# Guest matmuls cut in halves, batch loops written out, and VectorE's guests moved between scans in a fused Mamba and attention kernel

## The chip, the cores and the metric

The kernel runs on 1 core of a Trainium2 chip. The metric is the device time of one execution in microseconds (us). The kernel before takes 3528.84 us, the median of three runs (3526.27 to 3528.93).

## What is computed

For each of B = 4 batches of a sequence x[512, 256], all in fp32:

```
h, gate = adaLN(x, c)                                  # layer norm, scale, shift
for each direction (forward, backward):
    xs, z = split(h @ in_w);  xs = silu(xs)            # 512 channels
    dt, B, C = split(xs @ xproj_w); dt = softplus(dt + dt_bias)
    hst[t] = hst[t-1] * exp(dt[t] * A) + dt[t] * xs[t] * B[t]   # 512 channels x 64 states
    y[t]   = sum over states of hst[t] * C[t];  y = (y + xs * D) * silu(z)
x = x + gate * (y_fwd @ out_w + y_bwd @ out_w)
x = x + gate * (silu(h @ w1) * (h @ w2)) @ w3           # h = adaLN(x, c)
x = x + gamma1 * attention(adaLN(x)) @ proj             # 16 heads, l2-normed q and k
x = x + gamma2 * gelu(adaLN(x) @ fc1) @ fc2
```

## The kernel before

The five engines each run one instruction list, and semaphores set the order between them; every order below is written out by hand. Each of the five runs `batch(b, False)` in a hardware loop `Fori(0, B - 1)` (three turns) and then `batch(B - 1, True)` once, written out. Inside the loop a wait compares with a register value; in the written-out batch it compares with a constant. `wait_over` is a semaphore that only gets incremented behind some waits.

**A batch.** It begins with the scan stage: 128 rows, 64 states forward (d = 0) and 64 backward (d = 1). A row is one state of all 512 channels, as four tiles k = 0..3 of 128 channels by 512 time steps. Per row:
- ScalarE (`feed_scan`, L637 to L643) makes three 128x512 pieces of the inflow and one small diagonal, then four decay tiles exp(dt * A).
- TensorE (`turn_inflow`, L851, L852) turns the inflow of tile k into a PSUM bank (two banks, so it waits until scan k - 2 is over), then `sum_up` (L860) adds the weighed states of the tile six places back into the output banks.
- VectorE (`scan_row`, L1226) runs the scan of each tile, four per row.
- GpSimd (`weigh`, L531) multiplies two scanned tiles at a time by the row of C, twice per row. C's rows come by DMA from SyncE's queue, two states at a time.

States and decays have two slots of a row each, so VectorE can be at most about two pairs of tiles ahead of GpSimd.

**Guests.** While the scan of one direction runs, the next direction's inputs are prepared in its rows. The tuples at the top say in which row s (0 to 63) of a direction each step stands: TensorE's guest matmuls of 512 columns in rows IN_AT (16 rows), C_AT (4 rows, 64 channels wide) and DT_AT (16 rows), one in each row; the B projection in rows 48 to 51, the turns of dtx in rows 52, 55, 56, 58. TensorE does its guest behind tile k == 1 of the row. VectorE's guests stand in 17 rows (L1175 in TANH_AT, L1178 in row 26, L1182 in DT_CAP_AT, L1187 in DT_READY_AT), behind all four scans of their row. GpSimd has four guests per direction (L514, DTX_AT). The last direction of the last batch prepares nothing.

**Look-ahead.** In the forward rows of the three looped batches the next batch's first layer norm is done as well (`look_ahead`): statistics in rows 8 to 11, x_norm in rows 16 to 19 (L1209, a tensor_scalar from SBUF to SBUF), a shift in row 25.

**After the scan** come the Mamba output, MLP, attention and a second MLP, with no scan beside them; a batch ends with an add on VectorE (L1139) and SyncE's store of `out` (L484). SyncE then issues the next batch's first rows of C (L415).

The functions that the diff touches, and their callers:

Of the kernel before, what the change touches and what calls it, by code (L numbers as in the profile page):

```python
# [11 lines left out]
P = 128  # L12
# [100 lines left out]
def build(nc, inp, out):  # L113
    ctx = ExitStack()
    with ctx:
# [122 lines left out]
        wait_over = sem("wait_over")  # L238

# [147 lines left out]
        def _(sp):  # L387
# [18 lines left out]
            def spill(n):  # L406

                sp.wait_ge(c_t_ready, n + 1)
                sp.dma_start(c_spill[bass.ds(n, 1)].rearrange("a m h (j l) -> (a m h j) l", l=L), c_t[:]).then_inc(c_spilled, 16)

            def spread_rows(b, r):
# [4 lines left out]
                             c_spill[bass.ds(n, 1), m, half, :].partition_broadcast(P)).then_inc(c_loaded[half], 16)  # L416
# [21 lines left out]
            def batch(b, last):  # L438

                for r in range(0, BATCH_ROWS, HALF):  # L440
                    d, at = r // NS, r % NS
                    if at == 0:
                        sp.wait_ge(c_spilled, (b * 2 + d + 1) * 16)
                        sp.sem_inc(wait_over, 1)
# [5 lines left out]
                    if d == 0 and at == 6:  # L450
                        sp.dma_start(gate[:].rearrange("p g d -> p (g d)"),
                                     gate_spill[bass.ds(b, 1), :].rearrange("b d -> (b d)").partition_broadcast(P)).then_inc(gate_loaded, 16)
                    if at == 30 and (d == 0 or not last):
                        spill(b * 2 + d + 1)
                    if at == 24 and (d == 0 or not last):
                        sp.wait_ge(in_mm, (b * 2 + d + 2) * 2 * KI)
                        sp.sem_inc(wait_over, 1)
# [5 lines left out]
                    if at == 54 and (d == 0 or not last):  # L463
                        sp.wait_ge(b_tok_mm, b * 2 + d + 2)
                        sp.sem_inc(wait_over, 1)
# [7 lines left out]
                if not last:  # L473

                    sp.wait_ge(lanes_turned, (b + 1) * NG)
                    sp.sem_inc(wait_over, 1)
# [9 lines left out]
            with sp.Fori(0, B - 1) as b:  # L486
                batch(b, False)
            batch(B - 1, True)
# [4 lines left out]
        def _(pool):  # L493
# [44 lines left out]
            def batch(b, last):  # L538
# [9 lines left out]
                pool.sem_inc(wait_over, 1)  # L548
                pool.memset(qk_pad[:], 0.0).then_inc(pads_zero, 1)
                pool.wait_ge(pads_zero, b + 1)  # L550
                pool.sem_inc(wait_over, 1)
# [8 lines left out]
            with pool.Fori(0, B - 1) as b:  # L560
                batch(b, False)
            batch(B - 1, True)


        @block.scalar
        def _(act):
# [7 lines left out]
            def ln(b, i):  # L574
# [4 lines left out]
                act.activation(h_t[:, 1, :], banks[1], ACT.Identity, bias=mod[:, i, SHIFT, 1, bass.ds(b, 1)],  # L579
                               scale=mod[:, i, SCALE, 1, bass.ds(b, 1)]).then_inc(ln_ready, 1)  # L580
# [37 lines left out]
            def look_ahead(b, s):  # L618

                if s == AHEAD_SHIFT_AT[1]:  # L620
                    act.wait_ge(ahead_turned, (b + 1) * KD)
                    act.activation(h_ssm[:, 1, :], guest[0], ACT.Identity, bias=mod[:, 0, SHIFT, 1, bass.ds(b, 1)],
                                   scale=mod[:, 0, SCALE, 1, bass.ds(b, 1)]).then_inc(h_high_ready, 1)
# [81 lines left out]
            with act.Fori(0, B - 1) as b:  # L705
                batch(b, False)
            batch(B - 1, True)
# [3 lines left out]
        def _(pe):  # L711
# [41 lines left out]
            def prepare(n, d, s, ahead=None, first=False):  # L753

                if s in IN_AT:
                    at = IN_AT.index(s)
                    m, kc = at // KD, at % KD
                    if at == 0:
                        pe.wait_ge(in_loaded, 16 * KD * (n + 1))
                    if kc == 0 and m < 2:  # L760
# [13 lines left out]
                    last = pe.matmul(guest[m % 2], lhs, rhs, start=(kc == 0), stop=(kc == KD - 1))  # L774
                    if kc == KD - 1:
                        last.then_inc(in_mm, 1)
                if s in C_AT:
                    kc = C_AT.index(s)
                    if kc == 0:
                        pe.wait_ge(xproj_loaded, 16 * KI * (n + 1))  # L780
                        pe.wait_ge(in_ready, n * 2 * KI + 2 * KI - 1)
                    last = pe.matmul(guest[0][0:NS, :], xproj_w[:, kc, DI + NS:DI + 2 * NS], xs[:, kc, :],
                                     start=(kc == 0), stop=(kc == KI - 1))
                    if kc == KI - 1:
                        last.then_inc(c_mm, 1)
                for m in range(KI):
                    if s in DT_AT[m]:
                        kc = DT_AT[m].index(s)
                        if kc == 0:
# [8 lines left out]
                            else:  # L798
                                pe.wait_ge(dt_ready, n * KI + m - 1)
                        last = pe.matmul(guest[(m + 1) % 2], xproj_w[:, kc, m * P:(m + 1) * P], xs[:, kc, :],  # L800
                                         start=(kc == 0), stop=(kc == KI - 1))
                        if kc == KI - 1:
                            last.then_inc(dt_mm, 1)
                if s in B_TOK_AT:
# [605 lines left out]
```

## Time and profile before

| | us |
|---|---|
| median of three runs | 3528.84 |
| the profiled execution | 3529.55 |
| its span, first to last instruction | 3527.8 |
| PE, DVE, ACT, POOL busy | 3275.1, 2823.1, 2734.3, 2487.5 |

PE is TensorE's matmul, PEld its weight load, DVE VectorE, ACT ScalarE, POOL GpSimd, SP SyncE. In a row of a timeline the second number is the length of the group from its first start to its last end, and the bracket tells how long the engine sat idle before it and what it waited for. Neighbouring instructions overlap slightly in the records, so rates are taken from start to start. The scan stages run from about 99 to 749, 966 to 1616, 1833 to 2484 and 2692 to 3317 us of the span. The mean granted TensorE clock is 0.963.

### The profile page before, as it was taken

The page shows a single profiled execution, that of the slowest core. Times are in us where ns is not written, and L with a number is a line of the kernel's source. Part 1 is how long each engine was busy: PE and PEld are TensorE (multiplying, and loading weights), DVE is VectorE, ACT ScalarE, POOL GpSimd, SP SyncE. Part 2 cuts the span into 40 slices and gives each one's busy share as a digit, 9 for nine tenths or more (in the row PEclk, how much of TensorE's full clock was granted, in tenths as well). Part 3 has the DMA queues.
Part 4 walks back from the last instruction along what each step waited for, and adds up shares of the span by engine and source line. Part 5 has one row for each costly group of instructions (what it writes and reads, how often), then busy time and mean ns, then how long its engine had stood idle before and what let it go on. Part 6 is the DMA issues. An engine that isn't in the chain of part 4 may idle for free.

```text
span 3527.8 us, 68244 instructions
## 1 busy us (share of the span) xinstructions
PE 3275.1 (93%) x22944; PEld 2605.5 (74%) x22944; DVE 2823.1 (80%) x3001; ACT 2734.3 (78%) x4713; POOL 2487.5 (71%) x1103
## 2 busy tenths in 40 slices
PE   7999999988799999998979999999798999999888
PEld 4778888864488888886458788888546888888744
DVE  2899999956299999995639999999455999999653
ACT  1989999952498999993349999999146999999523
POOL 1789999950098999993019999999203999999600
PEclk9999999997999999999889999999989999999989
DMA  3221212100111121110011211212002211111000
GB/s 127 82 68 49 70 55 68 60 26 13 48 65 62 55 70 54 63 67 25 1 59 60 68 53 66 67 57 67 13 1 75 66 56 61 60 55 57 29 13 7
DMA packets 56732, 186.83 MB, mean 53 GB/s; under 512 B 6577, under 2 KB 12721, under 8 KB 55473
## 3 DMA queue, kind: packets, MB, share of 16 engines
q1 hardware_dynamic: 56370, 182.26, 15.3%
q8 instruction: 195, 3.19, 0.4%
q14 instruction: 167, 1.37, 0.1%
HBM read 179.08 MB, written 3.16 MB: 52 GB/s over the span
## 4 chain that ended last, share of the span: by engine, by line
POOL 47%; issue 25%; PE 24%; DVE 3%; DMA 1%; POOLq 0%; ACT 0%; SPq 0%; DVEq 0%; ACTq 0%
POOL states L531 45%; PE bank L993 3%; PE bank L860 3%; PE bank L851 3%; PE bank L900 2%; PE bank L1012 2%; PE bank L1074 2%; PE bank L1024 2%; PE bank L852 1%; PE bank L774 1%; PE bank L800 1%; POOL part L514 1%; PE bank L963 1%; PE bank L736 0%; PE bank L944 0%
## 5 line engine op out<-in xcount | busy, mean ns | idle before, releaser
L531 POOL TENSOR_TENSOR states<-states,c_rows 128x1024 f32<-128x1024 f32 x1024 | 2401.5, 2380 | 566.3 <-DMA c_rows<-c_spill 293.0
L1226 DVE TENSOR_TENSOR_SCAN states<-decay,bank 128x512 f32<-128x512 f32 x2048 | 2336.4, 1201 | 152.8 <-PE bank L852 106.1
L643 ACT ACTIVATE decay<-dt,a_log 128x512 f32<-128x512 f32 x2048 | 1305.5, 710 | 0.0
L860 PE MATMUL bank<-ident,states 128*128 128x128 f32 x8192 | 1240.5, 275 | 34.6 <-POOL states L531 11.9
L851 PE MATMUL bank<-ident,inflow_tok 128*128 128x128 f32 x6144 | 1070.3, 283 | 63.1 <-DVE states L1226 54.3
L637 ACT ACTIVATE inflow_tok<-dtx_tok,b_tok 128x512 f32<-128x512 f32 x1536 | 995.3, 712 | 134.7 <-PE bank L852 134.2
L860 PEld LDWEIGHTS bank<-ident,states 128*128 128x128 f32 x8192 | 952.5, 142 | 76.7 <-POOL states L531 73.4
L851 PEld LDWEIGHTS bank<-ident,inflow_tok 128*128 128x128 f32 x6144 | 686.7, 141 | 361.6 <-issue 127.1
L852 PE MATMUL bank<-b_diag,dtx_tok 128*128 128x128 f32 x4096 | 794.5, 276 | 0.0
L852 PEld LDWEIGHTS bank<-b_diag,dtx_tok 128*128 128x128 f32 x4096 | 621.3, 192 | 0.0
L638 ACT ACTIVATE b_diag<-ident,b_tok 128x128 f32<-128x128 f32 x512 | 199.3, 389 | 0.0
L1313 DVE TENSOR_REDUCE decay<-bank 128x1 f32<-128x512 f32 x256 | 159.0, 684 | 46.2 <-PE bank L993 45.7
L558 POOL TENSOR_TENSOR states<-inflow_tok 128x512 f32<-128x512 f32 x16 | 16.7, 1041 | 240.3 <-DVE inflow_tok L1280 240.3
L993 PE MATMUL bank<-dtx_tok,dt 32*128 32x512 f32 x512 | 169.4, 808 | 6.8 <-DVE decay L1313 3.7
L693 ACT ACTIVATE y_gated<-bank 128x512 f32<-128x512 f32 x176 | 91.7, 601 | 63.5 <-PE bank L1012 63.5
L1012 PE MATMUL bank<-dt,dtx_tok 32*128 32x512 f32 x512 | 130.6, 673 | 0.0
L800 PE MATMUL bank<-xs,xproj_w 128*128 128x512 f32 x256 | 128.7, 594 | 0.0
L993 PEld LDWEIGHTS bank<-dtx_tok,dt 32*128 32x128 f32 x512 | 72.6, 230 | 67.0 <-DVE decay L1313 42.8
L1161 DVE TENSOR_TENSOR dt<-bank,row_b 128x512 f32<-128x512 f32 x16 | 11.0, 687 | 126.0 <-PE bank L900 126.0
L577 ACT ACTIVATE std<-var_eps 128x4 f32<-128x4 f32 x12 | 2.5, 205 | 141.0 <-DVE var_eps L1125 141.0
L749 PE MATMUL bank<-ident,x_norm 128*128 128x128 f32 x96 | 23.0, 413 | 60.0 <-DVE x_norm L1130 60.0
L1012 PEld LDWEIGHTS bank<-dt,dtx_tok 32*128 32x128 f32 x512 | 53.6, 199 | 26.0 <-issue 10.8
(143 smaller groups left out, 1968.6 us busy)
## 6 DMA issues: line engine op xcount, KB each, us to landing
c_rows<-c_spill SPq DMA_DIRECT2D x256, 512.0 KB, 3.7
xproj_w<-in_xproj_w SPq DMA_DIRECT2D x32, 320.0 KB, 4.3
in_w<-in_in_w SPq DMA_DIRECT2D x16, 512.0 KB, 4.8
in_w<-in_fc_w SPq DMA_DIRECT2D x8, 512.0 KB, 5.3
xproj_w<-in_w SPq DMA_DIRECT2D x8, 512.0 KB, 5.0
xproj_w<-in_fc_w SPq DMA_DIRECT2D x4, 1024.0 KB, 4.8
y_gated<-in_mod_w SPq DMA_DIRECT2D x1, 2048.0 KB, 7.6
x_ahead<-in_x SPq DMA_DIRECT2D x4, 512.0 KB, 5.1
```

The lines of the kernel that those rows point to most:

```text
L531: pool.tensor_tensor(pair, pair, c_row, ALU.mult).then_inc(weighed, 1)
L637: act.activation(inflow_tok[:, r % SLOTS, t, :], dtx_tok[:, d, t, :], ACT.Copy, scale=b_tok[:, d, t, s:s + 1])
L638: act.activation(b_diag[:, r % SLOTS, :], ident[:], ACT.Copy, scale=b_tok[:, d, TT - 1, s:s + 1]).then_inc(inflow_tok_ready, 1)
L643: act.activation(decay[:, r % SLOTS * KI + k, :], dt[:, d, k, :], ACT.Exp, scale=a_neg[:, d, k, s:s + 1]).then_inc(decay_ready, 1)
L800: last = pe.matmul(guest[(m + 1) % 2], xproj_w[:, kc, m * P:(m + 1) * P], xs[:, kc, :], start=(kc == 0), stop=(kc == KI - 1))
L851: pe.transpose(to[:, t * P:(t + 1) * P], inflow_tok[:, r % SLOTS, t, k * P:(k + 1) * P], ident[:])
L852: pe.matmul(to[:, (TT - 1) * P:TT * P], dtx_tok[:, d, TT - 1, k * P:(k + 1) * P], b_diag[:, r % SLOTS, :], start=True, stop=True).then_inc ...
L860: last = pe.matmul(banks[KI + t][:, k * P:(k + 1) * P], states[:, r % SLOTS * KI + k, t * P:(t + 1) * P], ident[:], is_transpose=True, sta ...
L993: pe.matmul(score_bank(u), q_t[a, g, t * P:(t + 1) * P], k_t[a, g, :], start=True, stop=True).then_inc(scores_mm, 1)
L1012: pe.matmul(banks[S_BANKS + v % T_BANKS], k_t[a, g, kt * P:(kt + 1) * P], q_t[a, g, :], start=True, stop=True).then_inc(scores_t_mm, 1)
L1226: dve.tensor_tensor_scan(states[:, slot, time], decay[:, slot, time], banks[k % INFLOW_BANKS][:, time], 0.0, ALU.mult, ALU.add).then_inc(s ...
L1313: dve.tensor_reduce(qk_pad[:, t, g, lane:lane + 1], score_bank(u), AX.X, ALU.min).then_inc(neg_ready, 1)
```

## The change

Four edits:
- TensorE's guest matmuls of 512 columns become two of 256. The first half is issued behind tile k == 1 and the second behind k == 3 of the same row; waits stay with the first half, the semaphore with the second. The B projection, the turns of dtx and of x_norm stay whole, behind k == 1.
- VectorE's scan guests and look-ahead stand between scan 1 and scan 2 of their row, no longer behind scan 3. The y gating of direction 0 stays behind all four scans.
- The look-ahead's x_norm is a scalar_tensor_tensor, with rstd as a broadcast SBUF tensor.
- All batches are written out on all engines; `wait_over` is gone.

```diff
-                with pe.Fori(0, B - 1) as b:          # and the same on SP, POOL, ACT, DVE
-                    batch(b, False)
-                batch(B - 1, True)
+                for b in range(B):
+                    batch(b, b == B - 1)
...
+            def halves(to, lhs, rhs, h, start, stop):
+
+                out = None
+                for half in h:
+                    c = slice(half * L // 2, (half + 1) * L // 2)
+                    out = pe.matmul(to[:, c], lhs, rhs[:, c], start=start and half == 0, stop=stop, skip_group_check=True)
+                return out
...
-                    last = pe.matmul(guest[m % 2], lhs, rhs, start=(kc == 0), stop=(kc == KD - 1))
-                    if kc == KD - 1:
+                    last = halves(guest[m % 2], lhs, rhs, h, kc == 0, kc == KD - 1)
+                    if kc == KD - 1 and 1 in h:
                         last.then_inc(in_mm, 1)
...
+                    if k % 2 and (d == 0 or not last):
+                        prepare(b * 2 + d + 1, 1 - d, s, (k // 2,), b + 2 if d == 0 and not last else None)
                     if k == 1:
-                        if d == 0 or not last:
-                            prepare(b * 2 + d + 1, 1 - d, s, b + 2 if d == 0 and not last else None)
                         if d == 0 and not last:
                             look_ahead(b + 1, s, b * 2 + 1)
...
-                    dve.tensor_scalar(x_norm[:, t, :], x_ahead[:, t, :], mean_var[:, t, 0:1], rstd[:, t:t + 1],
-                                      ALU.subtract, ALU.mult).then_inc(ahead_norm, 1)
+                    dve.scalar_tensor_tensor(x_norm[:, t, :], x_ahead[:, t, :], mean_var[:, t, 0:1],
+                                             rstd[:, t:t + 1].to_broadcast([P, D]), ALU.subtract,
+                                             ALU.mult).then_inc(ahead_norm, 1)
...
-                    scan_row(b, r)
-                    if d == 1 and s == 0:
-                        gate_rows(b, 0)
+                    scan_row(b, r, range(0, PAIR))
                     if d == 0 or not last:
...
                         prepare(b * 2 + d + 1, 1 - d, s)
                     if d == 0 and not last:
                         look_ahead(b + 1, s)
+                    scan_row(b, r, range(PAIR, KI))
+                    if d == 1 and s == 0:
+                        gate_rows(b, 0)
```

## Rows read from the trace of the kernel before

**Rows 1.** The page, costliest group: count | busy, mean ns | idle before.

```profile
L531 POOL TENSOR_TENSOR states<-states,c_rows 128x1024 f32<-128x1024 f32 x1024 | 2401.5, 2380 | 566.3 <-DMA c_rows<-c_spill 293.0
```

**Rows 2.** Windows: stretch, its length; PE, PEld, DVE, ACT, POOL busy (x); clock, DMA.

```profile
3020.00:3310.00 290.00, 276.18 (x2254) 249.03 (x2254) 287.04 (x250) 284.33 (x491) 287.45 (x124) 1.00 0.16 56
1305.00:1612.00 307.00, 301.70 (x2356) 259.29 (x2355) 290.81 (x266) 294.37 (x510) 294.12 (x128) 1.00 0.18 60
```

**Rows 3.** Windows of line 1226 alone: each from scan 0 of row 3 to row 52.

```profile
983.22:1236.29 253.07, 223.29 (x197) 0.99 0.17 60
1311.19:1556.33 245.14, 222.35 (x198) 1.00 0.17 58
2708.88:2956.05 247.17, 222.80 (x197) 1.00 0.18 61
```

**Rows 4.** Timeline of DVE, looped batches: start us, us, instructions [idle <-releaser].

```profile
215.47 4.55 DVE L1226 TENSOR_TENSOR_SCAN states<-decay,bank 128x512 f32<-128x512 f32 x4 [0.78 <-PE bank L852]
...
1341.43 6.77 DVE L1226 TENSOR_TENSOR_SCAN states<-decay,bank 128x512 f32<-128x512 f32 x6
...
1443.88 4.55 DVE L1226 TENSOR_TENSOR_SCAN states<-decay,bank 128x512 f32<-128x512 f32 x4 [0.49 <-PE bank L852]
...
1455.61 0.72 DVE L1182 TENSOR_SCALAR part<-bank,dt_b 128x512 f32<-128x512 f32 x1
1456.26 11.21 DVE L1226 TENSOR_TENSOR_SCAN states<-decay,bank 128x512 f32<-128x512 f32 x10
```

**Rows 5.** Timeline of DVE, the written-out last batch.

```profile
2837.57 4.55 DVE L1226 TENSOR_TENSOR_SCAN states<-decay,bank 128x512 f32<-128x512 f32 x4 [0.55 <-ACT decay L643]
```

**Rows 6.** Timeline of PE around one guest matmul, last batch.

```profile
2744.93 0.30 PEld L774 LDWEIGHTS bank<-in_w,h_ssm 128*128 128x128 f32 x2
...
2745.90 0.49 PE L851 MATMUL bank<-ident,inflow_tok 128*128 128x128 f32 x3
...
2746.89 0.49 PE L851 MATMUL bank<-ident,inflow_tok 128*128 128x128 f32 x3
```

**Rows 7.** Lines by form: GpSimd's guest, and the look-ahead's x_norm.

```profile
L514 POOL TENSOR_TENSOR part<-dt,xs 128x512 f32<-128x512 f32 x32 | 41.2, 1288 | 38.2 <-DVE dt L1187 38.2
...
L1209 DVE TENSOR_SCALAR x_norm<-x_ahead,mean_var,rstd 128x256 f32<-128x256 f32 x16 | 17.4, 1102 | 1.2 <-POOL rstd L520 1.2
```

**Rows 8.** Timeline of DVE and POOL at the look-ahead's x_norm, first batch.

```profile
205.78 2.22 DVE L1209 TENSOR_SCALAR x_norm<-x_ahead,mean_var,rstd 128x256 f32<-128x256 f32 x1
...
193.34 14.52 POOL L531 TENSOR_TENSOR states<-states,c_rows 128x1024 f32<-128x1024 f32 x6 [2.47 <-DVE states L1226]
```

**Rows 9.** Timeline of DVE and SP where batch 1 and batch 3 begin.

```profile
957.04 0.69 DVE L1139 TENSOR_TENSOR part<-part,x_norm 128x512 f32<-128x512 f32 x1
965.52 2.33 DVE L1226 TENSOR_TENSOR_SCAN states<-decay,bank 128x512 f32<-128x512 f32 x2 [7.79 <-issue]
...
958.24 0.42 SPq L484 DMA_DIRECT2D out<-part  x1
965.23 0.99 SPq L415 DMA_DIRECT2D c_rows<-c_spill  x2
...
2691.02 0.69 DVE L1139 TENSOR_TENSOR part<-part,x_norm 128x512 f32<-128x512 f32 x1
2691.63 5.66 DVE L1226 TENSOR_TENSOR_SCAN states<-decay,bank 128x512 f32<-128x512 f32 x5
```

**Rows 10.** Timeline of DVE: the last scans of batches 0 and 3, and the last add.

```profile
740.12 4.75 DVE L1226 TENSOR_TENSOR_SCAN states<-decay,bank 128x512 f32<-128x512 f32 x4
...
3307.37 5.67 DVE L1226 TENSOR_TENSOR_SCAN states<-decay,bank 128x512 f32<-128x512 f32 x5 [0.36 <-ACT decay L643]
...
3523.68 0.69 DVE L1139 TENSOR_TENSOR part<-part,x_norm 128x512 f32<-128x512 f32 x1
```

**Rows 11.** Timeline of ACT and DVE: one tanh and the instruction that reads it.

```profile
1349.23 0.58 ACT L597 ACTIVATE part<-bank 128x512 f32<-128x512 f32 x1
...
1355.38 0.66 DVE L1175 SCALAR_TENSOR_TENSOR xs<-part,bank 128x512 f32<-128x512 f32 x1
```

More of the change, by code:

```diff
@@ L558, in batch @@
                     pool.tensor_tensor(qk_sq[:, t, :], qk[:, t, :], qk[:, t, :], ALU.mult).then_inc(sq_ready, 1)
-            with pool.Fori(0, B - 1) as b:
-                batch(b, False)
-            batch(B - 1, True)
+            for b in range(B):
+                batch(b, b == B - 1)
         @block.scalar
@@ L703, in batch @@
                     act.activation(gelu_h[:, m, :], banks[m], ACT.Gelu, bias=fc1_b[:, m:m + 1]).then_inc(fc1_ready, 1)
-            with act.Fori(0, B - 1) as b:
-                batch(b, False)
-            batch(B - 1, True)
+            for b in range(B):
+                batch(b, b == B - 1)
         @block.tensor
@@ L751, in ln, with prepare @@
                 pe.wait_ge(ln_ready, (n + 1) * KD)
-            def prepare(n, d, s, ahead=None, first=False):
+            def halves(to, lhs, rhs, h, start, stop):
[4 more added lines that the diff above has]
+                return out
+            def prepare(n, d, s, h=(0, 1), ahead=None, first=False):
                 if s in IN_AT:
@@ L778, in prepare @@
                     kc = C_AT.index(s)
-                    if kc == 0:
+                    if kc == 0 and 0 in h:
                         pe.wait_ge(xproj_loaded, 16 * KI * (n + 1))
                         pe.wait_ge(in_ready, n * 2 * KI + 2 * KI - 1)
-                    last = pe.matmul(guest[0][0:NS, :], xproj_w[:, kc, DI + NS:DI + 2 * NS], xs[:, kc, :],
-                                     start=(kc == 0), stop=(kc == KI - 1))
-                    if kc == KI - 1:
+                    last = halves(guest[0][0:NS, :], xproj_w[:, kc, DI + NS:DI + 2 * NS], xs[:, kc, :], h, kc == 0, kc == KI - 1)
+                    if kc == KI - 1 and 1 in h:
                         last.then_inc(c_mm, 1)
@@ L799, in prepare @@
                                 pe.wait_ge(dt_ready, n * KI + m - 1)
-                        last = pe.matmul(guest[(m + 1) % 2], xproj_w[:, kc, m * P:(m + 1) * P], xs[:, kc, :],
-                                         start=(kc == 0), stop=(kc == KI - 1))
-                        if kc == KI - 1:
+                        last = halves(guest[(m + 1) % 2], xproj_w[:, kc, m * P:(m + 1) * P], xs[:, kc, :], h, kc == 0,
+                                      kc == KI - 1)
+                        if kc == KI - 1 and 1 in h:
                             last.then_inc(dt_mm, 1)
+                if 0 not in h:
+                    return
                 if s in B_TOK_AT:
@@ L1079, in batch @@
                 residual_rows(lambda c, t: gelu_h[:, c, t * P:(t + 1) * P], lambda c: fc2_w[:, c, :], KF)
-            with pe.Fori(0, B - 1) as b:
-                batch(b, False)
-            batch(B - 1, True)
+            for b in range(B):
+                batch(b, b == B - 1)
         @block.vector
@@ L1342, in batch @@
                 residual(b, 3, GAMMA2, FC2_B)
-            with dve.Fori(0, B - 1) as b:
-                batch(b, False)
-            batch(B - 1, True)
+            for b in range(B):
+                batch(b, b == B - 1)
 def kernel(**inputs):
```

42 lines of the change are left out of this document (17 added, 25 removed).

## The prediction, made blind

> **What bounds the kernel now.** I read the page first. GpSimd's weighing, 1024 times 2.38 us, is 2401.5 of 3527.8 us [rows 1], and the chain of waits names it for most of the scan. The windows show where it really is the bound. In the last direction, which has no guests, POOL is busy for 287.45 of 290 us with 124 weighings: 290/124 = 2.34 us each, 4.67 us a row [rows 2]. That is the floor of a row, and GpSimd's four guests of 1.29 us add about 5 us to each of the seven directions that prepare the next one [rows 7]. In such a direction POOL is busy only 294 of 307 us [rows 2].
>
> To see who holds it there I cut windows on VectorE's scans, 49 rows (3 to 51): 253.07 us forward with look-ahead, 245.14 backward, both in looped batches, and 247.17 in the written-out batch [rows 3]. The floor would be 49 x 4.67 + 5 = 234. VectorE's timeline explains the rest. Ten scans with nothing between take 11.21 us, 1.11 from start to start (a record overlaps the next by 0.08), so an empty row is 4.45 [rows 4], below the floor. To that come:
> - its own guest, 0.58 (0.66 less the overlap) [rows 11] or 0.65 for dt [rows 4];
> - a wait where TensorE's guest matmul was ahead of scan 2: 0.49 idle in the loop, hence a row of 4.55 + 0.49 = 5.04; 0.78 where the matmul is 64 channels wide, 5.33 [rows 4]; 0.55 in the written-out batch, 5.10 [rows 5].
>
> With both, a row is 5.6 to 5.7. But the six scans from 1341.43 go through without an idle time [rows 4], though the first four are row 9, which has a guest matmul: VectorE's guest at the end of row 8 gave TensorE 0.58 us to run ahead. So today a VectorE guest covers the TensorE guest of the next row, in nine rows of a direction (4, 9, 12, 17, 20, 27, 35, 42, 44), and by the same the B projection in 48 and 51.
>
> **Halves.** A half costs half. In the written-out batch the guest's weights load at 2744.93 and the next tile's matmuls start at 2745.90, 0.97 later, while two weight loads take 0.30 and the following tile comes 0.99 after [rows 6]. A tile costs TensorE 0.99 at full speed, and I put the guest at 0.86 and a half at 0.43. The whole guest of 0.86 delays the scan by 0.55 + 0.08 = 0.63, so 0.23 is slack and a half should delay it by 0.20. Two halves by VectorE: 4.45 + 0.40 = 4.85. By TensorE: 4 x 0.99 + 0.86 = 4.82. I take 4.82. Bounds: 4.67, the floor, if the slack takes them whole, and 5.10 if the second costs as much as the first saves.
> The 64-channel matmul delays by 0.78 + 0.08, 0.29 more than the 0.57 of the others in the loop. I take this as fixed for each insertion, so that two halves give a TensorE row of 4 x 0.99 + 0.86 + 0.58 = 5.40, nothing won.
>
> **VectorE's guests between scans 1 and 2.** They now stand where the first half's delay falls, and leave TensorE time for the second. A row with both guests becomes 4.45 + 0.58 = 5.03 (dt: 5.10). The price is the cover of the next row: those nine rows go from about 4.46 to 4.82, and 48 and 51 to 5.1.
> GpSimd gets its second pair later by the guest. That costs nothing where VectorE is the slower one, and its lead of up to two pairs covers it elsewhere. What the guests read is there: a tanh of ScalarE ends at 1349.81 and is read at 1355.38 [rows 11], and reading two scans (2.2 us) sooner, with the matmul's last half about 2.2 later, leaves over 1 us. ScalarE is busy 294 of 307 us already [rows 2], so it would be late next.
>
> The ledger of 49 rows, without look-ahead: 8 rows with a guest of 0.58 (TensorE's hidden) 40.2; 8 with one of 0.65, 40.8; row 22 (both, 64 channels) 5.3; 20 with halves only 96.4; 3 with 64-channel halves only 16.2; 3 with the B projection only, uncut, 15.3; 6 empty 26.8. Sum 241.0, above the floor of 234.
> - Three looped backward directions (I take the measured one for all): 245.14 - 241.0 = 4.14, times 3: 12.4.
> - The last batch's forward: 247.17 - 241.0 = 6.2.
> - Three forward ones: look-ahead is the difference 253.07 - 245.14 = 7.9 and stays (see x_norm below): 12.4 again.
> Sum 31. Written-out code costs 247.17 against 245.14 before; that is inside the ledger, which is built with the 0.63 of the written-out batch. Rows 0 to 2 and 52 to 63 I leave at nothing: the first are held by the skip terms on TensorE, the last by GpSimd.
>
> **x_norm as scalar_tensor_tensor.** In the scan the second x_norm of 2.22 us ends at 208.00, when GpSimd's six weighings from 193.34 end at 207.86 [rows 8]: it sat until GpSimd was through, and GpSimd then idled 2.47 for its scans. The sixteen take 17.4 us [rows 7]; four of them ran before the scan. With 1.7 for those four, (17.4 - 1.7)/3 = 5.2 per forward direction, against about 1.3 if none had to wait. No row shows a VectorE instruction with two SBUF tensors beside GpSimd; all others in the scan have one operand in PSUM. Bounds: 0 and 3.9 x 3 = 12 us. The nearest row is L1209 itself, the only one with nothing in PSUM, so I take 0.
> The Trainium skill, "SBUF — State Buffer", "Who interferes with whom", says that a VectorE instruction with two SBUF inputs also holds the port pair that GpSimd reads by, and the later one blocks until the first is over. By it the new form waits as the old one did, a gain of 0; the trace agrees for the old form (2.22 against GpSimd's end) and shows nothing of the new.
>
> **Loops written out.** Batch 1 begins by the loop's jump: last add at 957.04, first scan at 965.52, 8.48 later, with 7.79 idle for nothing that the profile shows; SyncE too has 6.99 between its store and the rows of C. Batch 3 begins by falling out of the loop: 2691.02 to 2691.63, 0.61 [rows 9]. So each jump costs VectorE 7.9 us. GpSimd's first weighing then waits for the rows of C, not for VectorE; but VectorE is the slower one for the 49 rows that follow, so its gain counts. Two jumps (the third turn falls through): 15.7.
> Waits on constants shorten the tail as well: last scan's end to last add is 957.04 - 744.87 = 212.2 in batch 0 and 3523.68 - 3313.04 = 210.6 in batch 3 [rows 9, 10]. Three looped tails at 1.3: 4. Before the scan, 36 guests run as two halves with no scan beside them: 1 lost at most.
>
> **Sum.** 31 + 15.7 + 4 - 1 = 50. The profiled execution took 3529.55, 0.7 above the median: 3529.55 - 50 - 0.7 = 3479.
>
> **Rivals.**
> 1. The new x_norm runs free: 12 us more, 3467. For it: one source per port and no fast mode. Against: all operands in SBUF.
> 2. Halves and moved guests cancel: the second half falls in a place with less slack (turn 0 of a row waits for two semaphores) and the nine lost covers eat the gain. Each direction stays at the written-out 247.17: six looped ones lose 2.0 each, so 15.7 + 4 - 12 = 8 gained, 3521.
> 3. Slower: a fixed cost per insertion, as the 64-channel one shows with 0.29. If each half carries it, TensorE's row is 4 x 0.99 + 2 x 0.72 = 5.40: the 20 rows of halves cost 0.58 more, 11 rows with both guests about 0.33 more, 15 per direction, 106 in seven, so 3585. It decides from f = 0.15 per half on: 20 x 2f + 11 x (2f - 0.2) = 50/7 = 7 us a direction. Against: the 0.86 of a whole guest leaves no room for it in 128-channel ones [rows 6].
> 4. The change does a little more than I count: halves vanish in the slack and rows go to the floor, 234 + a few: 5 per direction, 35 in all, 3444.
>
> **Chances.** Forecast 0.48, rival 1 0.22, rival 2 0.13, rival 3 0.07, rival 4 0.10. Within 0.2% (7 us, about what a measurement of this kernel can tell from no change) lies a third of rival 2. Faster 0.88, same 0.05, slower 0.07. The range from 3446 to 3512 holds the first two, nearly all of 4 and the near side of 2.
>
> **What would show it.** The two idle times near 7.8 us before a batch's first scan are gone. The 49-row windows read 241 (backward) and 249 (forward). Waits for line 852 before a scan are many and short, about 0.1 to 0.2, with rows of 4.82. x_norm still has members near 2 us; if all are 0.33, rival 1 holds. If rows with halves take 5.1 or more, my half is wrong; if ScalarE's decay becomes the releaser of scans with idle times over 0.3, I missed the next bound.

## The result, and the profile after

The changed kernel takes 3478.35 us (median of 4 runs, 3474.93 to 3479.61), the kernel before 3527.56 beside it: ratio 0.9862, 95% interval 0.9847 to 0.9878. I had said 3479.0. The profiled execution took 3479.61, its span is 3477.8 against 3527.8, 50.0 less, at the same clock of 0.963.

The page's two groups that mattered, count | busy, mean ns | idle before:

```profile
L524 POOL TENSOR_TENSOR states<-states,c_rows 128x1024 f32<-128x1024 f32 x1024 | 2402.2, 2381 | 512.2 <-DMA c_rows<-c_spill 424.4
L1224 DVE TENSOR_TENSOR_SCAN states<-decay,bank 128x512 f32<-128x512 f32 x2048 | 2351.7, 1203 | 86.1 <-PE bank L852 27.4
```

GpSimd's weighing is as long as before [rows 1], and it idles 54 us less. By the view of waits its idle time for VectorE's scans falls from 271.7 to 77.1 us and that for the rows of C rises from 293.0 to 424.4, but most of this is a name: one of the three long waits between batches (141.4 us) was put down to VectorE's scans before and to the rows of C after. Without it the scans' share falls from 130.3 to 77.1.

The windows from scan 0 of row 3 to row 52, cut on the scan's line as in [rows 3]: stretch, length, DVE busy, clock, DMA:

```profile
965.73:1211.97 246.24, 224.76 (x196) 1.00 0.19 64
1286.53:1528.34 241.81, 224.89 (x196) 1.00 0.17 58
2662.49:2904.24 241.75, 224.99 (x196) 1.00 0.19 63
```

Cut so in every batch, with all that lies between, the span's 50.0 us come from here:

| stretch | before | after | gained |
|---|---|---|---|
| forward, batches 0 to 2 | 251.69, 253.07, 251.68 | 247.71, 246.25, 247.92 | 14.6 |
| forward, last batch | 247.17 | 241.75 | 5.4 |
| backward, batches 0 to 2 | 245.13, 245.14, 245.14 | 241.65, 241.81, 241.97 | 10.0 |
| backward, last batch (no guests) | 226.96 | 226.88 | 0.1 |
| rows 0 to 2, eight directions | 149.3 | 145.9 | 3.4 |
| rows 52 to 63, eight directions | 439.1 | 437.9 | 1.1 |
| last add to first scan | 8.48, 8.78, 0.61 | 0.61, 0.61, 0.61 | 16.0 |
| last scan's start to last add's start, four tails | 851.8 | 852.6 | -0.8 |

The rest, 0.1, is prologue and end. TensorE's granted clock moves some of these numbers. In batch 1 before, it stood at the lower of its two levels, 1.2 GHz, for 3.4 us of rows 17 and 18 (5.57 and 5.65 us, against 4.83 and 4.97 in batch 0); this is why that window reads 253.07 and the other two 251.7. After, the same happened in batches 0 and 2, at rows 19 and 20, and not in batch 1. So the forward windows without it go from 251.7 to 246.2 us. Of the 3.4 us in rows 0 to 2, 2.0 are batch 2's, whose first rows stood at the lower level for 7.8 us before and not at all after.

The length of a row is read from its scans, from start to start. Four rows of the backward direction, with all engines (PE, PEld, DVE, ACT, POOL busy): row 10 (two halves), row 11 (a VectorE guest alone), row 21 (64-channel halves), row 48 (B projection, whole):

```profile
1320.64:1325.46 4.82, 4.82 (x43) 4.62 (x42) 4.67 (x4) 4.82 (x9) 4.72 (x3) 1.00 0.28 94
1325.46:1330.53 5.07, 4.48 (x39) 3.95 (x37) 5.07 (x6) 5.07 (x10) 4.75 (x3) 1.00 0.05 17
1374.37:1379.77 5.40, 5.40 (x43) 4.29 (x41) 4.67 (x4) 5.40 (x10) 5.04 (x4) 1.00 0.05 18
1507.98:1513.07 5.09, 5.05 (x46) 4.77 (x45) 4.56 (x5) 4.68 (x10) 4.92 (x3) 1.00 0.27 96
```

In a row of halves PE is busy for all of 4.82 us and VectorE isn't; in a row with a VectorE guest it is the other way round. VectorE's timeline from row 3 on answers to [rows 4]:

```profile
1288.78 0.66 DVE L1173 SCALAR_TENSOR_TENSOR xs<-part,bank 128x512 f32<-128x512 f32 x1
1289.36 14.22 DVE L1224 TENSOR_TENSOR_SCAN states<-decay,bank 128x512 f32<-128x512 f32 x12
1303.50 0.66 DVE L1173 SCALAR_TENSOR_TENSOR xs<-part,bank 128x512 f32<-128x512 f32 x1
1304.08 8.99 DVE L1224 TENSOR_TENSOR_SCAN states<-decay,bank 128x512 f32<-128x512 f32 x8
```

In these rows there is no idle time to read any more. Twelve scans in a row took 14.22 us, where 12 at the undisturbed 1.11 take 13.4: TensorE's halves show as scans that start 0.03 or 0.16 later than 1.11 us after the one before, which the timeline doesn't print as a wait. The many short waits for line 852 that I had forecast are therefore not in the view (32 in all, 27.4 us), though the rows are as long as I said. So a group of scans is read by its length over its count.

Where batch 1 begins, against [rows 9]:

```profile
947.95 0.69 DVE L1137 TENSOR_TENSOR part<-part,x_norm 128x512 f32<-128x512 f32 x1
948.55 2.32 DVE L1224 TENSOR_TENSOR_SCAN states<-decay,bank 128x512 f32<-128x512 f32 x2
```

And the look-ahead, against [rows 8]: DVE from row 16 to 20 of batch 1, then POOL over the same stretch.

```profile
1031.76 0.66 DVE L1173 SCALAR_TENSOR_TENSOR silu_z<-part,bank 128x512 f32<-128x512 f32 x1
1032.34 1.22 DVE L1206 SCALAR_TENSOR_TENSOR x_norm<-x_ahead,mean_var,rstd 128x256 f32<-128x256 f32 x1
1033.48 4.54 DVE L1224 TENSOR_TENSOR_SCAN states<-decay,bank 128x512 f32<-128x512 f32 x4
1037.94 0.59 DVE L1206 SCALAR_TENSOR_TENSOR x_norm<-x_ahead,mean_var,rstd 128x256 f32<-128x256 f32 x1
...
1047.90 0.65 DVE L1173 SCALAR_TENSOR_TENSOR silu_z<-part,bank 128x512 f32<-128x512 f32 x1
1048.48 2.33 DVE L1206 SCALAR_TENSOR_TENSOR x_norm<-x_ahead,mean_var,rstd 128x256 f32<-128x256 f32 x1
```

```profile
1028.57 21.95 POOL L524 TENSOR_TENSOR states<-states,c_rows 128x1024 f32<-128x1024 f32 x9
1053.13 2.37 POOL L524 TENSOR_TENSOR states<-states,c_rows 128x1024 f32<-128x1024 f32 x1 [2.60 <-DVE states L1224]
```

The view merges GpSimd's weighings. Asked at single moments, it shows the one that is under way when the second norm starts, the one behind it, and the one under way when the fourth starts:

```profile
1035.88 2.37 POOL L524 TENSOR_TENSOR states<-states,c_rows 128x1024 f32<-128x1024 f32 x1
1038.20 2.56 POOL L524 TENSOR_TENSOR states<-states,c_rows 128x1024 f32<-128x1024 f32 x1
1048.18 2.35 POOL L524 TENSOR_TENSOR states<-states,c_rows 128x1024 f32<-128x1024 f32 x1
```

The fourth norm ends at 1050.81, this weighing at 1050.53: 0.28 later. The second ends at 1038.53 (37.94 + 0.59), its weighing at 1038.25: 0.28 later too. So all four norms of a scan wait, the short ones as well, each for what is left of the weighing under way: 2.05 us for the fourth, 0.31 for the second. The same 0.28 or 0.29 us holds for all 84 norms of this form beside a scan, in seven traces. A weighing that follows at once is held in its turn: 2.56 us in place of 2.37. Behind the fourth norm GpSimd idled 2.60 for the scans.

A long norm costs more than itself. TensorE stands still behind it, and then its granted clock may fall (batch 0, stretch, length, PE, PEld, DVE, ACT, POOL busy, clock, DMA):

```profile
200.50:203.30 2.80, 0.00 (x0) 0.00 (x0) 2.80 (x3) 2.80 (x6) 1.28 (x1) 1.00 0.00 0
203.60:207.00 3.40, 3.40 (x19) 3.40 (x18) 2.54 (x3) 1.29 (x2) 2.36 (x1) 0.50 0.00 0
```

In the twelve traces of this case there are 14 stretches at the lower level that begin in rows 3 to 63. Each begins 2.8 to 5.1 us after the start of a norm of over 2 us; not every such norm is followed by one.

### The profile page after: what moved, and what is told of

Its sections match the earlier page's. It is cut to its first block and busy times, and to the rows that moved or that the text cites. A ratio compares the mean times of both kernels' runs of the same rounds, so it can differ in the third digit from the quotient of the medians.

```text
span 3477.8 us, 59778 instructions
## 1 busy us (share of the span) xinstructions
PE 3238.9 (93%) x23520; PEld 2700.6 (78%) x23520; DVE 2836.8 (82%) x3001; ACT 2727.7 (78%) x4712; POOL 2488.4 (72%) x1103
## 5 line engine op out<-in xcount | busy, mean ns | idle before, releaser
L524 POOL TENSOR_TENSOR states<-states,c_rows 128x1024 f32<-128x1024 f32 x1024 | 2402.2, 2381 | 512.2 <-DMA c_rows<-c_spill 424.4
L1224 DVE TENSOR_TENSOR_SCAN states<-decay,bank 128x512 f32<-128x512 f32 x2048 | 2351.7, 1203 | 86.1 <-PE bank L852 27.4
L851 PE MATMUL bank<-ident,inflow_tok 128*128 128x128 f32 x6144 | 1044.0, 279 | 52.8 <-DVE states L1224 42.6
L851 PEld LDWEIGHTS bank<-ident,inflow_tok 128*128 128x128 f32 x6144 | 706.1, 141 | 232.3 <-issue 120.7
L747 PE MATMUL bank<-xs,xproj_w 128*128 128x256 f32 (+1 forms) x640 | 187.6, 385 | 0.0
L1012 PE MATMUL bank<-dt,dtx_tok 32*128 32x512 f32 x512 | 130.3, 674 | 0.0
L747 PEld LDWEIGHTS bank<-xs,xproj_w 128*128 128x128 f32 (+1 forms) x640 | 92.5, 180 | 12.9 <-issue 10.2
L747 PE MATMUL bank<-h_ssm,in_w 128*128 128x256 f32 x256 | 77.4, 396 | 1.0 <-ACT h_ssm L612 1.0
```

The lines of the kernel that those rows point to most:

```text
L524: pool.tensor_tensor(pair, pair, c_row, ALU.mult).then_inc(weighed, 1)
L747: out = pe.matmul(to[:, c], lhs, rhs[:, c], start=start and half == 0, stop=stop, skip_group_check=True)
L851: pe.transpose(to[:, t * P:(t + 1) * P], inflow_tok[:, r % SLOTS, t, k * P:(k + 1) * P], ident[:])
L1012: pe.matmul(banks[S_BANKS + v % T_BANKS], k_t[a, g, kt * P:(kt + 1) * P], q_t[a, g, :], start=True, stop=True).then_inc(scores_t_mm, 1)
L1224: dve.tensor_tensor_scan(states[:, slot, time], decay[:, slot, time], banks[k % INFLOW_BANKS][:, time], 0.0, ALU.mult, ALU.add).then_inc(s ...
```

## The experiments

In all of them the kernel before ran beside, at 3525.66, 3527.39 and 3527.26 us median in the three sets. Windows are the 49 rows as above.

**1. Written out alone.** The kernel after with whole guests behind tile k == 1, VectorE's guests behind the row, x_norm as before:

```
-  if k % 2 ...: prepare(..., (k // 2,), ...)
+  if k == 1 ...: prepare(..., (0, 1), ...)      # one 512-column matmul
-  scan_row(b, r, range(0, PAIR)); guests; scan_row(b, r, range(PAIR, KI))
+  scan_row(b, r, range(0, KI)); guests
```

> The kernel before with its batch loops written out and nothing else (whole guest matmuls behind tile k == 1, VectorE's guests behind scan 3, x_norm as tensor_scalar). My theory: the two pauses of 7.8 us before a batch's first scan go (16 us, and about 3 more in rows 0 to 2), but each looped direction's 49 rows take the written-out pace, 247.2 us backward in place of 245.1, so about 12 us come back: 3522 us, 0.998 of before. Rival, that the written-out form costs nothing in the rows: 49 rows stay at 245.1 and the time is 3509.

Measured: 3519.64 us, ratio 0.9982 (0.9972 to 0.9992), 6.0 us less than before. Batch 1's backward window:

```profile
1304.51:1552.04 247.53, 1.00 0.17 57
```

Both jumps are gone (0.61), 16 us; but the backward windows are 247.19 to 247.53 where the loop had 245.14, and the forward ones 253.3 to 253.8 against 251.7 (253.1 in batch 1, with its stretch at the lower clock). Written out, these windows are about 2 us longer while TensorE's whole guest sets them, 10.8 in the six, which gives back most of the 16.

**2. The guests behind the row.** The kernel after, VectorE's guests behind the fourth scan again (second part of the edit above).

> The changed kernel with VectorE's guests back behind scan 3 of their row; halves and written-out loops stay. My theory: with halves TensorE's own work (4.82 us in a row with a guest) sets the pace in either order, and a VectorE guest gives TensorE 0.6 us wherever it stands, so the 49 rows stay at 241 to 242 us and the time within 4 us of 3478. Rival, that the place between the scans is what hides the first half: 11 rows with both guests cost 0.2 to 0.3 more, 49 rows take 244 to 245 and the time is about 3500.

Measured: 3472.26 us, ratio 0.9849 (0.9833 to 0.9866). The windows:

```profile
1285.89:1527.66 241.77, 224.80 (x196) 1.00 0.18 58
2658.30:2899.74 241.44, 225.00 (x196) 1.00 0.19 63
```

They are those of the kernel after (241.81, 241.75). The rows differ, the sum doesn't: a row with both guests is 5.24 or 5.30 in place of 5.07 and 5.13, the next 4.66 in place of 4.83. The intervals of the two ratios overlap, so the 6 us between the medians are not a gain that these runs establish. Of 7.1 us between the spans 4.5 lie in the four tails, which stood at the lower clock for 235.5 us in the kernel after and for 218.5 here. My rival here, 3500, fell: the cover moves, it isn't lost.

**3. Whole guests in the new order.** The first part of the edit alone: `if k == 1: prepare(..., (0, 1), ...)`, one matmul of 512 columns.

> The changed kernel with whole guest matmuls behind tile k == 1 in the scan; VectorE's guests stay between scans 1 and 2 and the loops written out. My theory: rows with both guests stay near 5.1 us, but the 20 rows with a TensorE guest alone take 5.10 in place of 4.82 with no cover from the row before: 49 rows take about 246.6 us and the time is about 3517. Rival, that moving VectorE's guests carries the gain and the halves add little: 49 rows 242 to 243, time about 3485.

Measured: 3516.43 us, ratio 0.9972 (0.9961 to 0.9984).

```profile
1300.69:1547.77 247.08, 222.60 (x197) 1.00 0.17 57
2693.83:2940.90 247.07, 222.60 (x197) 1.00 0.18 61
```

A row of one whole guest is 5.10. Against the kernel after each backward or last forward window is 5.3 us longer, and the time 38 us: this is what the halves bring. Against run 1, whose guests stand behind the row and whose x_norm is the old one, the backward windows are 0.2 us shorter in the mean: with whole guests too the move is worth next to nothing.

**4. The loops back.** The kernel before with the halves, the moved guests and the new x_norm, its batches in the loop.

```
-  for b in range(B): batch(b, b == B - 1)
+  with engine.Fori(0, B - 1) as b: batch(b, False)
+  batch(B - 1, True)
```

> The changed kernel with the hardware loop over the first three batches back; halves, moved guests and the new x_norm stay. My theory: the pauses of 7.8 us come back twice, and 3 us in rows 0 to 2, while the 49 rows keep 241 to 242 us because TensorE's work binds them and not the latency of a wait: about 3497 us. Rival, that the loop's cheaper waits (0.055 us less at each late scan) show in the rows as well: 49 rows about 238 us, 3480.

Measured: 3493.57 us, ratio 0.9907 (0.9891 to 0.9924), 15 us more than the kernel after. DVE where batch 1 begins:

```profile
946.73 0.69 DVE L1150 TENSOR_TENSOR part<-part,x_norm 128x512 f32<-128x512 f32 x1
954.93 2.33 DVE L1238 TENSOR_TENSOR_SCAN states<-decay,bank 128x512 f32<-128x512 f32 x2 [7.51 <-issue]
```

The jumps are back (8.21 and 7.61). The backward windows are 240.75 or 240.76, 0.9 to 1.2 less than written out. The 15.7 us between the two spans are 14.6 in the jumps and 5.7 in the tails, less 6.2 in the six looped windows, and 1.6 elsewhere.

The Trainium skill, "Runtime: NRT & Kernel Launch", "Instruction fetch mechanics", says that a taken branch to outside the fetched window waits for a fetch by DMA. The trace agrees with that as far as it goes: 7.51 us in which the engine waited for nothing shown, only at the turns that jump, while the batch that falls out of the loop starts after 0.61. No run here shows the fetch itself.

**5. x_norm as before.** In the kernel after:

```
-  dve.scalar_tensor_tensor(x_norm[:, t, :], x_ahead[:, t, :], mean_var[:, t, 0:1],
-                           rstd[:, t:t + 1].to_broadcast([P, D]), ALU.subtract, ALU.mult)
+  dve.tensor_scalar(x_norm[:, t, :], x_ahead[:, t, :], mean_var[:, t, 0:1], rstd[:, t:t + 1],
+                    ALU.subtract, ALU.mult)
```

> The kernel after with one edit undone: x_norm is written by tensor_scalar again in place of scalar_tensor_tensor with a broadcast second input. My theory: both forms read the tile over VectorE's second input path or wait for GpSimd in the same way, so the four norms of a forward scan last as long as in the kernel after (1.1 to 1.2, 0.5, 0.5 and 2.3 us, against 2.31, 0.44, 0.39 and 2.22 before), and the time stays at 3478 us, within 2. Rival: the changed form is what made the first norm shorter and what it saves is 1.1 us or more of a forward scan; then undoing it costs 3 to 12 us, 3481 to 3490. A first norm of 2.3 us again in row 16 would speak for the rival.

Measured: 3473.90 us, ratio 0.9849 (0.9832 to 0.9865). The lines by form, the kernel after and then this one:

```profile
L1206 DVE SCALAR_TENSOR_TENSOR x_norm<-x_ahead,mean_var,rstd 128x256 f32<-128x256 f32 x16 | 15.8, 1005 | 1.2 <-POOL rstd L513 1.2
```

```profile
L1206 DVE TENSOR_SCALAR x_norm<-x_ahead,mean_var,rstd 128x256 f32<-128x256 f32 x16 | 13.9, 887 | 1.2 <-POOL rstd L513 1.2
```

Its DVE timeline in batch 1, first, second and fourth norm:

```profile
1031.12 1.09 DVE L1206 TENSOR_SCALAR x_norm<-x_ahead,mean_var,rstd 128x256 f32<-128x256 f32 x1
...
1036.59 0.46 DVE L1206 TENSOR_SCALAR x_norm<-x_ahead,mean_var,rstd 128x256 f32<-128x256 f32 x1
...
1046.87 2.19 DVE L1206 TENSOR_SCALAR x_norm<-x_ahead,mean_var,rstd 128x256 f32<-128x256 f32 x1
```

The waits are the same, as I held. What I had not expected is that the old form is the shorter one: each norm ends 0.15 us after GpSimd's weighing, where the new form takes 0.28. Where GpSimd stands still, in the four norms before the scan, it is 0.41 against 0.48. So the changed form costs 0.13 a norm, 0.54 us a forward window (247.17, 245.70, 247.39 against 247.71, 246.25, 247.92). The rest of the 4.4 us is outside the windows, and the intervals overlap with those of the kernel after.

**6. x_norm in other rows.** In the kernel after:

```
-  AHEAD_NORM_AT = (16, 17, 18, 19)
+  AHEAD_NORM_AT = (17, 18, 20, 21)
```

> The kernel after with the four x_norm instructions in rows 17, 18, 20 and 21 of a forward scan in place of 16 to 19, so that none stands behind a tanh guest. My theory: a norm is long only where it starts after GpSimd's weighing of the row has begun (2.5 us after the row's first scan); behind a tanh guest of 0.58 us it does, alone it does not. Row 16 then falls from 6.18 to about 5.07 us, row 19 from 7.29 to 5.07, row 20 rises from 4.83 to 4.98, row 21 stays at 5.40 since TensorE bounds it: 3.1 us less in each of three forward scans, 3469 us. Rival: the length belongs to the instruction and its data (the last of the four, or the tile), wherever it stands; then the 2.3 us move with it, and the time stays at 3478 us, within 3.

Measured: 3464.92 us, ratio 0.9825 (0.9808 to 0.9841). DVE of batch 1, then POOL:

```profile
1031.72 1.41 DVE L1206 SCALAR_TENSOR_TENSOR x_norm<-x_ahead,mean_var,rstd 128x256 f32<-128x256 f32 x1
...
1037.52 0.59 DVE L1206 SCALAR_TENSOR_TENSOR x_norm<-x_ahead,mean_var,rstd 128x256 f32<-128x256 f32 x1
...
1047.54 0.59 DVE L1206 SCALAR_TENSOR_TENSOR x_norm<-x_ahead,mean_var,rstd 128x256 f32<-128x256 f32 x1
...
1052.51 0.58 DVE L1206 SCALAR_TENSOR_TENSOR x_norm<-x_ahead,mean_var,rstd 128x256 f32<-128x256 f32 x1
```

```profile
1023.48 21.64 POOL L524 TENSOR_TENSOR states<-states,c_rows 128x1024 f32<-128x1024 f32 x9
```

The fourth norm is 0.58 now, with the same tile as the 2.33 before: the length belongs to the moment, not to the instruction. The first norm misses: GpSimd is still in the weighing that began at about 30.50 (23.48 + 3 x 2.34) and ends at 32.85, 0.28 before the norm does. My account of the moment was not quite right: a short norm doesn't start while GpSimd is free. It starts in the last 0.3 us of a weighing, and a tanh guest of 0.58 us in front of it carries it past the start of the next one.

The forward windows are 243.68, 243.81 and 243.86, 10.5 us less in sum, where I had 9.3. Only 4.7 us of it are shorter norms (14.2 to 9.5 us in the three scans). Batch 1, which had no stretch at the lower clock in either kernel, gained 2.4 and not 3.1; the other two gained 4.0 and 4.1, and in their rows, with no norm of over 2 us left, there is no such stretch any more.

**7. Quarters.** In the kernel after, four pieces of 128 columns, one behind each tile's turn (only the guests of IN_AT, C_AT and DT_AT):

```
-  c = slice(half * L // 2, (half + 1) * L // 2)
+  c = slice(half * L // 4, (half + 1) * L // 4)
-  if k % 2 ...: prepare(..., (k // 2,), ...)
+  prepare(..., (k,), ...)
```

> The kernel after with every guest matmul of the scan cut in four pieces of 128 columns, one at each of the row's four places, in place of two of 256. My theory: a row with guests is bound by TensorE's sum, 4 x 0.99 + 0.86 = 4.82 us, which four pieces leave as it is; rows stay at 4.82 us with four intervals of about 1.2 in place of 1.14 and 1.27, a backward window of 49 rows at 241 to 243 us, and the time at 3478 us, within 4; the 64-channel rows may rise, by 0.29 us for each further piece (+0.6 us in 4 rows of each of 7 scans, up to 16 us, 3494). Rival: a guest costs only what its single visit exceeds the slack of 0.2 us between a scan and its inflow; then 0.215 us pieces are free, the rows fall to about 4.46 us, a window to about 234 us and the time to 3425 us.

Measured: 3499.47 us, ratio 0.9925 (0.9908 to 0.9942). Row 10, row 21 and the whole backward window:

```profile
1328.87:1333.71 4.84, 4.84 (x47) 4.84 (x45) 4.84 (x5) 4.84 (x10) 4.73 (x3) 1.00 0.30 89
1382.73:1388.73 6.00, 6.00 (x47) 4.64 (x45) 4.88 (x5) 5.46 (x11) 5.02 (x4) 1.00 0.08 25
1294.63:1539.33 244.70, 239.81 (x2063) 225.13 (x2062) 238.47 (x214) 236.22 (x410) 234.67 (x102) 1.00 0.17 58
```

**8. Half the columns.** In the kernel after, each half works out the first 128 of its 256 columns, and the rest of the next direction's projections is left out.

```
-  c = slice(half * L // 2, (half + 1) * L // 2)
+  c = slice(half * L // 2, (half + 1) * L // 2 if h == (0, 1) else half * L // 2 + L // 4)   # (0, 1): outside the scans
```

> The kernel after, in which each of the two halves of a guest matmul inside the scans works out only the first 128 of its 256 columns; it leaves out half of the columns of the next scan's projections. My theory: the price of a half is its columns, 0.43 us for 256 and 0.215 for 128; TensorE's sum of a row is then 4 x 0.99 + 0.43 = 4.39 us, below VectorE's four scans of 1.11, and each visit is within the slack of 0.2 us: rows of halves alone fall from 4.82 to about 4.46 us, 64-channel rows from 5.40 to about 4.97, rows with a VectorE guest stay at 5.07 and 5.13. Some 19 rows x 0.36 + 4 x 0.43 = 8.5 us less in each of seven windows of 49 rows (241.8 to 233.3 us backward), 3418 to 3430 us. Rival: a visit has a fixed price that does not depend on its columns; then rows stay at 4.82 us and the time at 3478 us, within 3. With the run in four quarters: the same piece of 128 columns, four of them in a row there and two here.

Measured: 3423.76 us, ratio 0.9709 (0.9693 to 0.9725). Row 10, row 25 and the backward window:

```profile
1296.47:1300.93 4.46, 4.46 (x42) 4.36 (x41) 4.46 (x5) 4.46 (x9) 4.46 (x3) 1.00 0.15 34
1367.59:1372.56 4.97, 4.97 (x43) 4.29 (x41) 4.66 (x4) 4.97 (x10) 4.88 (x4) 1.00 0.40 133
1263.50:1497.76 234.26, 226.61 (x1931) 210.12 (x1929) 230.62 (x214) 234.23 (x410) 232.65 (x102) 1.00 0.17 60
```

Read 7 and 8 together. The same piece of 128 columns stands in a row four times in the one and twice in the other: 4.84 and 4.46 us. Pieces that small would be free in both if only the single visit counted; a fixed price per visit would show in both. What counts is TensorE's sum (four pieces 0.86, two 0.43), and once it is below VectorE's four scans the pieces are free. The 64-channel rows go 4.97, 5.40, 6.00: from 4 x 0.99 = 3.96 that is 1.01, 1.44 and 2.04, two pieces of 0.22 + 0.29, two of 0.43 + 0.29, and four of 0.22 + 0.29. So each piece of 64 channels has a fixed price of 0.29, and a piece of 128 channels none: four cost the 0.86 of two, within 0.02. The 64-channel rows are 2.3 of the 2.9 us by which the quarters' window is longer, and most of why the run came 21 us above the kernel after, as its expectation allowed and not as its first number said.

**9 and 10. What the runs point to.** The kernel after with x_norm in rows 17, 18, 20, 21 by tensor_scalar, and the two kinds of TensorE guests that stood whole cut in two as well; then the same with VectorE's guests behind the row.

```
-  if 0 not in h: return
-  for kc in range(KI):                              # B projection, rows 48 to 51
+  for kc in [kc for kc in range(KI) if kc // 2 in h]:
-  for t in range(TT):                               # transposes of dtx, rows 52 to 58
+  for t in [t for t in range(TT) if t // 2 in h]:
```

> The kernel after with what the runs so far point to: x_norm in rows 17, 18, 20 and 21 and written by tensor_scalar (3464.9 us measured for the first, 1.6 us off for the second), and the two kinds of TensorE guests that still stood in one place cut in two as well: the B projection of rows 48 to 51 (one visit of 0.8 us: rows 48, 49 and 51 go from 5.09 to 4.82 us, -0.8 us a scan) and the transposes of dtx of rows 52, 55, 56 and 58 (a visit of 0.43 us: rows 52, 55 and 56 from 4.67 to 4.46 us, -0.6 us a scan). My theory: GpSimd weighs a row in 4.67 us and is at most about a row behind, so in rows 52 to 58 the transposes' part is lost to it: 3463.3 - 7 x 0.8, 3457 us. Rival: GpSimd has room, both parts come: 3453 us. Second rival: cut B projections lose as 64-column weights did in four pieces (0.29 us for each further piece), nothing is gained, 3463 us.

> The same edits with VectorE's guests behind the row's fourth scan, as in the run with the guests behind the row (3472.3 us, 6 less than the kernel after). My theory: the norm in row 19 falls from 2.3 us to about 0.4 (-1.9 x 3) and the form gives 1.6 us, B projection and dtx transposes as in the other kernel (-5.6): 3472.3 - 12.9, 3459 us; the place of the guests is worth less than the norms, so both orders end within 4 us of each other. Rival: the gain of the guests behind the row (6 us) adds to all of the other kernel's: 3451 us.

Measured: 3459.32 us, ratio 0.9808 (0.9795 to 0.9821), and 3458.11, ratio 0.9807 (0.9793 to 0.9820). Both beat before and after; against each other they are the same, so the second order adds nothing of its own. The first one's backward window and its rows 52 to 63:

```profile
1278.03:1518.88 240.85, 236.70 (x1931) 215.72 (x1929) 234.09 (x213) 235.83 (x410) 233.29 (x102) 1.00 0.16 58
1518.88:1573.52 54.64, 52.92 (x442) 48.55 (x440) 54.17 (x47) 51.27 (x91) 54.64 (x25) 1.00 0.21 69
```

Rows 48, 49 and 51 are 4.77, 4.75 and 4.76 in place of 5.09, 1.0 us of the window. Of that, 0.5 us is given back in rows 52 to 63 (54.64 against 54.12): POOL is busy for all of them, and the halved transposes bring nothing there. This was my theory for it: GpSimd's 4.67 us a row is the bound of these rows.

## Why the prediction was right, point by point

- **The halves: right, and now shown.** Rows of halves are 4.82, as TensorE's sum said, and runs 7 and 8 separate the sum from the single visit. The bounds I kept were not it: neither 4.67 nor 5.10. The 64-channel rows are 5.40 as worked out. The ledger gave 241.0 for 49 rows; measured 241.65 to 241.97 backward and 241.75 in the last batch. The 0.7 to 1.0 that it lacks lie in row 22, 5.40 and not 5.3; in rows with a VectorE guest, 5.07 and 5.13 in most and not 5.03 and 5.10, 0.4 in all; and in late scans, in other rows in each batch (batch 1: rows 12 and 27, 4.90 and 5.18), on which more below.
- **Sizes of the 31: right by two errors that cancelled.** The 241.0 was 0.8 low, four times. The forward directions came to 247.3 in the mean and not 248.9, and they started from 252.15 and not from batch 1's 253.07, which I had taken for all three though [rows 3] gives its clock as 0.99: 0.7 more a direction. 31 - 3.2 + 2.1 = 29.9.
- **VectorE's guests between scans: right as far as it went.** 5.07 and 5.13 for a row, 4.83 for the next. But the price of the lost cover eats the whole of it, and with halves the move is worth nothing (run 2): 5.07 + 4.83 = 9.90 against 5.24 + 4.66 = 9.90.
- **x_norm: right, 0 to a small loss.** It waits as before [rows 8]. The Trainium skill, "SBUF — State Buffer", "Who interferes with whom", has both forms blocked, the one by its two SBUF inputs, the other where it uses both ports, and the one that starts first has the pair for its whole instruction. Runs 5 and 6 agree: each norm that meets a weighing with more than 0.2 us to go ends 0.15 us (the old form) or 0.28 us (the new one) after it, and the next weighing is longer by up to 0.2. My reason for taking 0 was weaker than that: x_norm is not the only instruction with nothing in PSUM. The look-ahead's bn_stats, on the same x_ahead tile, was in the trace of before and takes its 0.42 us in the middle of a weighing, so L1209's wait doesn't follow from its operands' place alone.
- **The jumps: right.** 15.7 forecast, 16.0 measured, and run 4 brings them back.
- **The tails: wrong.** I had put 4 us to waits on constants; they came out 0.8 us longer. The step that failed took one difference (212.2 against 210.6) [rows 9, 10] for the cost of the loop. The tail from the last scan's start to the last add's start is 213.40, 213.43, 213.08 and 211.84 before, 212.94, 212.04, 213.44 and 214.17 after: the same written-out instructions vary by 2 us. They vary with the granted clock. By the traces' clock records the written-out tails of all runs take 211.4 us in the mean where the clock stood at the lower level for 51.2 us of them (8 tails), 211.6 at 54.6 us (12), 212.7 at 58.0 (13) and 213.8 at 61.4 (9). The six looped ones take 213.1 and 213.4 at 54.6, 213.4 at 58.0, and 214.5 to 214.9 at 61.4. So the loop does seem to cost about 1 us a tail, near the 1.3 that I had; but the kernel after stood at the lower level for 235.5 us of its four tails and the kernel before for 221.9, which would take it back. This is read from rows; no run set the clock. A tail's time at the lower level was not in the sum.
- **Left at nothing, or put at a loss:** rows 0 to 2 gave 3.4 us and rows 52 to 63 1.1; the 1 us that I took off for the time before the scan did not show (first scan at 99.57 us, 99.68 before).
- **The total: partly luck.** Halves 31 and 29.9, jumps 15.7 and 16.0 are the forecast. That the rest, put at 3, came out at 4 is several misses that cancelled.

Rival 2 (cancelling, 3521), rival 3 (a price per insertion, 3585) and rival 4 (3444) fell with runs 3, 7 and 8; rival 3 is real for 64 channels alone, 0.29 us. Rival 1 (a free x_norm) fell as such; by the place of the instruction (run 6) 10.5 us were to be had, near its 12, but less than half of them from the norms' own length. The stated range began at 3446, above rival 4's 3444, so it did not hold "nearly all" of that rival.

Still open: why written-out code makes the 49 rows 2 us longer with whole guests (run 1) and 1 us with halves (run 4). Where it does is in the traces. A scan that waits for TensorE starts 0.04 us after the end of its tile's last matmul in the looped batches of before and of run 4, and 0.09 in the written-out batches of these two, of the kernel after and of runs 1 and 3; this is the 0.49 against 0.55 of [rows 4, 5] (there the profile names ScalarE's decay, which ended within 0.01 us of that matmul). Rows of 4.82, which TensorE's sum sets, are the same in both. Besides, up to four scans in a written-out direction start about 0.45 us after the matmul, and none in a looped batch. In the last direction of before, which has no guests, it is every 64th scan (in rows 14, 30, 46 and 62), and in other directions most stand in the same rows whichever of the kernels it is. So this part goes with the place in the instruction list. No run changed the form of the waits alone, so why a start takes longer is not shown.

## What to carry to other kernels

Cut a guest only until the row takes no more than its engine's sum: here two pieces did that, and four gained nothing and cost the fixed price where a piece has one. Before a VectorE instruction that reads and writes SBUF is rewritten, see when it starts against GpSimd's, one instruction at a time and not in a merged group: moved by two rows it fell from 2.33 to 0.58 us, rewritten it gained nothing. Read the clock of a window before its length is taken for all others like it. Take the price of a loop from the turn itself, and compare its body written out too: here 16 us of jumps were won, and in the body 6 of them (with halves) or 11 (with whole guests) were paid back.

## What the runs showed of the hardware that I had not expected

- Beside a GpSimd weighing, tensor_scalar on 128x256 with both scalars per partition ends 0.15 us after the weighing, scalar_tensor_tensor with a broadcast second input 0.28 us after it, whatever was left of it when they started, from 0.2 to 2.1 us. With GpSimd still they take 0.41 and 0.48 us.
- A bn_stats on the same x_ahead tile, behind a tanh guest, begun at 1007.80 while GpSimd was weighing (three from 1002.63 to 1009.82), took its usual 0.42 us; x_norm in the same position took 2.33. DVE, then POOL of the kernel after:

```profile
1007.80 0.42 DVE L1194 BATCH_NORM_STATS2 stats<-x_ahead 128x6 f32<-128x256 f32 x1
```

```profile
1002.63 7.19 POOL L524 TENSOR_TENSOR states<-states,c_rows 128x1024 f32<-128x1024 f32 x3
```

- A matmul with 64 stationary channels in a stream of 128x128 ones has a fixed price of 0.29 us per piece whatever its columns (256 or 128), and 128-channel pieces have none within 0.02.
- A scan that waits for TensorE starts 0.04 us after the tile's last matmul in a looped batch and 0.09 in a written-out one.
- A norm of 2.3 us on VectorE left TensorE idle for at least 2.80 us, and its granted clock then stood at 1.2 GHz for 3.4 us; the two windows where this happened after are 1.5 and 1.7 us longer than the one where it didn't.
- A tail of about 213 us varies from 211.0 to 214.2 us with the same written-out instructions, and with it the time at the lower clock, from 51.2 to 61.4 us.
